# Expert weights split in another slot's step, and a PSUM bank for the z transposes, in a fused attention and mixture-of-experts block

## What is computed

```python
xn = _layernorm(x)
# attention: causal softmax over 256 keys, heads of 16, then Wo and bo
# experts:
scores = sigmoid(xn @ gate_w.T) + bias
topk_w, topk_idx = top_k(scores, 4)
topk_w = topk_w / (sum(topk_w) + 1e-20)
g = einsum('th,eih->eti', xn, Wg);  u = einsum('th,eih->eti', xn, Wu)
z = silu(g) * u
out = einsum('eti,ehi->th', z * cw.T[:, :, None], Wd)
out = out + silu(xn @ Sg.T) * (xn @ Su.T) @ Sd.T
return x + attention(xn) + out
```

## Time and profile before

| | us |
|---|---|
| median of 3 runs (565.2 to 567.9) | 566.04 |
| profiled execution, device time | 569.64 |
| its span | 567.9 |
| loop over slots in it, from the first row transpose to the last output projection | 134 to 554 |

### The profile page before, as it was taken

The page is one execution under the profiler, slowest core; times in us unless marked ns, Lnnn a source line. Parts: engine busy times, 40 slices in busy tenths (PEclk is TensorE's granted clock), DMA queues, the critical chain, the costliest instruction groups (busy, mean ns, idle before and its releaser), DMA issues.

```text
span 567.9 us, 9993 instructions
## 1 busy us (share of the span) xinstructions
PE 468.4 (82%) x2968; PEld 344.9 (61%) x2968; DVE 365.0 (64%) x606; ACT 263.5 (46%) x386; POOL 268.3 (47%) x234
## 2 busy tenths in 40 slices
PE   0995789968989997789878878997978899889880
PEld 0964578846667775367656655765656557667650
DVE  7377874676567957375779871787775546766510
ACT  2531212216555655165668642655736335645610
POOL 2002593304764652267546863573757336364510
PEclk9997999987998998899999899998989999889976
DMA  7804963336666557465687883668655534334222
GB/s 285 329 28 111 226 231 100 107 118 214 158 130 152 113 104 212 142 157 96 141 236 190 277 162 60 154 139 205 175 104 107 95 56 83 68 54 81 38 38 37
DMA packets 32060, 78.23 MB, mean 138 GB/s; under 512 B 4288, under 2 KB 11200, under 8 KB 28800
## 3 DMA queue, kind: packets, MB, share of 16 engines
q0 software_dynamic: 11936, 27.53, 26.8%
q1 hardware_dynamic: 17808, 43.96, 23.5%
q10 hardware_dynamic: 2256, 6.03, 5.0%
HBM read 54.04 MB, written 23.33 MB: 136 GB/s over the span
## 4 chain that ended last, share of the span: by engine, by line
PE 45%; DVE 15%; issue 8%; DMA 8%; ACT 8%; ACTq 6%; POOL 5%; SPq 2%; DVEq 1%; POOLq 1%
PE psum L1093 24%; PE psum L1221 5%; DMA q_parts<-stage 3%; ACT wsplit L573 3%; DVE negm L906 3%; PE psum L1187 2%; PE psum L1203 2%; POOL xn L446 2%; PE psum L1058 2%; ACTq L266 2%; PE psum L1115 2%; PE psum L1042 2%; POOL out L457 1%; PE psum L1103 1%; ACTq L264 1%
## 5 line engine op out<-in xcount | busy, mean ns | idle before, releaser
L1093 PE MATMUL psum<-wsplit,xgT 128*128 (+1 forms) x660 | 175.0, 416 | 0.2
L1093 PEld LDWEIGHTS psum<-wsplit,xgT 128*128 128x128 f32 x660 | 125.8, 197 | 30.3 <-issue 2.7
L457 POOL DMA_INDIRECT out<-ysb,tab x48 | 88.6, 1845 | 105.1 <-ACT ysb L606 84.2
L1093 PE MATMUL psum<-wsplit,zT 128*128 (+1 forms) x336 | 95.3, 420 | 29.0 <-DVE zT L898 29.0
L1093 PEld LDWEIGHTS psum<-wsplit,zT 128*128 128x128 f32 x336 | 61.6, 193 | 48.9 <-issue 37.6
L948 DVE TENSOR_TENSOR xgT<-psum,xgT 128x512 fp32r<-128x512 f32 x47 | 32.3, 688 | 65.4 <-ACT xgT L569 65.3
L437 POOL DMA_INDIRECT xg<-xn_rows,tab x47 | 51.9, 1104 | 29.6 <-PE psum L1231 20.0
L648 ACT ACTIVATE xn<-psum 128x1536 f32<-128x1536 f32 x32 | 46.5, 1453 | 40.6 <-PE psum L1189 40.6
L975 DVE TENSOR_TENSOR plo<-xn,phi 128x1536 f16<-128x1536 f32 x32 | 63.5, 1984 | 1.0
L446 POOL TENSOR_SCALAR_AFFINE_SELECT xn<-xn 128x512 f32<-128x512 f32 x64 | 55.3, 1060 | 7.9 <-ACT xn L648 7.8
L462 POOL TENSOR_TENSOR wsplit<-wraw,wsplit (+1 forms) x16 | 39.1, 2446 | 41.1 <-ACT wsplit L573 41.1
(11 more groups left out here) (180 smaller groups left out, 655.9 us busy)
## 6 DMA issues: line engine op xcount, KB each, us to landing
wraw<-wexp SPq DMA_DIRECT2D x17, 1024.0 KB, 6.1
wraw<-wexp SPq DMA_DIRECT2D x17, 512.0 KB, 4.6
q_parts<-stage SPq DMA_DIRECT2D x16, 192.0 KB
q_pack<-q_parts ACTq DMA_DIRECT2D x6, 384.0 KB, 4.6
xn<-x SPq DMA_DIRECT2D x4, 512.0 KB, 5.2
xn_rows<-xn SPq DMA_DIRECT2D x8, 256.0 KB, 7.6
ctxs<-x SPq DMA_DIRECT2D x8, 256.0 KB, 3.2
out<-ysb SPq DMA_DIRECT2D x8, 256.0 KB, 3.2
```

The costliest lines, as they stand in the source:

```text
L457: nc.gpsimd.indirect_dma_start(out=out, out_offset=rows_of(s), in_=ysb[:, par, :], in_offset=None, compute_op=ALU.add).then_inc(y_out[par] ...
L1093: last = MM(dst, lhs(a, k), split_weights(place, w, c), start=m == 0, stop=m == len(products) - 1)
```

## The change

The table's row 2 now holds, where a slot is the first of expert e, the number e+2, that is the number of the next expert, and 0 for expert 15 and for slots that start none. The gate and up weights of expert e+1 are split in the step of e's first slot: on ACT behind `high16` and ahead of `y_evac` (`gate_up_high`), on DVE behind `low16` at the end of the step (`gate_up_low`). The down weights of that expert follow in the next slot's step, on ACT behind the gate and up halves, if there are any, and on POOL where `down_low_of` stood. A register is loaded once in a slot on each of these engines, behind tanh or `gated`, and kept for the next slot; the parity is worked out from it. `x_high`, `z_high`, `x_low` and `z_low` stand in no branch any more. z is transposed into bank 3, and the wait of PE for y moves from ahead of the z transpose to ahead of `down`. The transposes of maxima in the loop go to bank 4, that of the attention products, with a wait for `csum_done` ahead of them and one for `nmT_sb` ahead of a batch's last `weighted`.

```diff
-        GU, XT, DN, PV = 5, 6, 7, 4
+        GU, XT, DN, PV = 5, 6, 7, 4
+        ZB, NM = 3, PV
...
-            def down_low_of(s):
+            def down_low_of(s, number):
+                if s == 1:
+                    down_low(1, 2)
+                elif s > 1:
+                    with pool.If(number > 0):
+                        down_low(bass.ds((number + 1) % 2, 1), number)
+                    pool.end_ifs()
...
+                        s = SPS * b + j
+                        number = first_of(s - 1) if 1 < s < NSLOT else None
+                        if s < NSLOT:
+                            down_low_of(s, number)
                         add_rows(b, j)
...
+            def gate_up_high(s, number):
+                if s == 0:
+                    weights_high(1, 2, HALVES[0], 0)
+                    weights_high(1, 2, HALVES[1], 0)
+                else:
+                    with act.If(number > 0):
+                        place = bass.ds((number + 1) % 2, 1)
+                        weights_high(place, number, HALVES[0], 0)
+                        weights_high(place, number, HALVES[1], 0)
+                    act.end_ifs()
...
-                        slot_parts(s, 1 - j % 2, not (last and j + 1 >= SPS - 1))
+                        if s + 1 < NSLOT:
+                            x_high(s + 1, 1 - par)
+                        z_high(s + (U1 - 1), 1 - par)
                         if j == BESIDE[g][-1] and (g == 3 or g == 7 and not last):
                             minus_maxima(2 * b + (g // 4 + 1), 1 - g // 4)
+                        if s < NSLOT:
+                            tanh(s + U1, par)
+                        number = first_of(s) if 0 < s < NSLOT else None
                         if j == BESIDE[g][0]:
                             high16(b, g)
+                        if s < NSLOT:
+                            gate_up_high(s, number)
+                            down_high(s, before)
                         y_evac(b, j)
+                        before = number
...
+                own.did(V.tensor_scalar(sexp[:, 0, :], sexp[:, 1, :], float(NE - 1), None, ALU.is_lt))
+                own.wait()
+                op(V.scalar_tensor_tensor(out=sexp_i[:, 2, :], in0=sexp[:, 1, :], scalar=2.0, in1=sexp[:, 0, :],
+                                          op0=ALU.add, op1=ALU.mult))
+                V.tensor_tensor(where[:, 2, :], sexp_i[:, 2, :], sexp_i[:, 1, :], ALU.mult).then_inc(slots_known, 1)
...
-                        slot_parts(s, 1 - j % 2, not (last and j + 1 >= SPS - 1))
-                        if not (last and j == SPS - 1):
+                        if s + 1 < NSLOT:
+                            x_low(s + 1, 1 - j % 2)
+                        z_low(s + (U1 - 1), 1 - j % 2)
+                        if s < NSLOT:
                             gated(s + U1, j % 2)
+                        number = first_of(s) if 0 < s < NSLOT else None
                         if j == BESIDE[g][0] and not (last and g >= 4):
                             maxima(G * b + (g + 4), (g + 4) % G)
                         if j == BESIDE[g][0]:
                             if g:
                                 context(b, g - 1)
                             low16(b, g)
+                        if s < NSLOT:
+                            gate_up_low(s, number)
...
-                        pe.wait_ge(y_sb, s + 1)
+                        if s == 0:
+                            pe.wait_ge(nmT_sb, 1)
                         z_transpose(s + (U1 - 1), 1 - j % 2)
                         if j == BESIDE[g][-1] and (g == 3 or g == 7 and not last):
+                            pe.wait_ge(csum_done, G * b + g + 1)
                             maxima_transpose(G * b + (g + 5), 1 - g // 4)
...
                         pe.wait_ge(w_low[1], prev[1])
+                        pe.wait_ge(y_sb, s + 1)
                         down(s + (U1 - 1), 1 - j % 2, prev[0])
...
                         elif g == G - 1:
+                            if not last:
+                                pe.wait_ge(nmT_sb, 2 * b + 3)
                             weighted(b, g)
```

More of the change, by code:

```diff
@@ L463, in down_low, with first_of @@
                                         wsplit[:, place, 0, PARTS[1]].bitcast(F32), ALU.subtract).then_inc(w_low[1], 1)
-            def down_low_of(s):
[L467 to L471, removed]
+            def first_of(s):
+                return pool.value_load(where[0:1, 2, s + 1:s + 2], min_val=0, max_val=NE)
+            def down_low_of(s, number):
[5 more added lines that the diff above has]
+                    pool.end_ifs()
             def add_attention(b):
@@ L573, in weights_high, with first_of, down_high @@
                 S(wsplit[:, place, 0, cols], wraw[:, place, cols], ACT.Copy).then_inc(w_high[part], 1)
[L575 to L599, removed]
+            def first_of(s):
+                return act.value_load(where[0:1, 2, s + 1:s + 2], min_val=0, max_val=NE)
+            def gate_up_high(s, number):
[8 more added lines that the diff above has]
+                    act.end_ifs()
+            def down_high(s, number):
+                if s == 1:
+                    weights_high(1, 2, PARTS[1], 1)
+                elif s > 1:
+                    with act.If(number > 0):
+                        weights_high(bass.ds((number + 1) % 2, 1), number, PARTS[1], 1)
+                    act.end_ifs()
             def y_evac(b, j):
@@ L659, in context_evac, with sequence @@
                     S(ctxT[:, qt, :, :], bank(qt).rearrange("p (k n) -> p k n", k=KD), ACT.Copy).then_inc(ct_sb, 1)
-            def sequence(b, last):
+            def sequence(b, last, before):
                 for g in range(G):
@@ L894, in shared_out, with z_low @@
                 V.tensor_tensor(ysb[:, n % 2, :], base[:, n % 2, :], bank(DN), ALU.add).then_inc(shared_done, 1)
-            def z_low(n, par, source=DN):
+            def z_low(n, par, source=ZB):
                 dve.wait_ge(zt_high, n + 1)
@@ L954, in gu_low, with first_of, gate_up_low @@
                                 wsplit[:, place, 0, HALVES[half]].bitcast(F32), ALU.subtract).then_inc(w_low[0], 1)
[L956 to L971, removed]
+            def first_of(s):
+                return dve.value_load(where[0:1, 2, s + 1:s + 2], min_val=0, max_val=NE)
+            def gate_up_low(s, number):
+                if s == 0:
+                    gu_low(1, 2, 0)
+                    gu_low(1, 2, 1)
+                else:
+                    with dve.If(number > 0):
+                        gu_low(bass.ds((number + 1) % 2, 1), number, 0)
+                        gu_low(bass.ds((number + 1) % 2, 1), number, 1)
+                    dve.end_ifs()
             def low16(b, g):
@@ L1123, in scores_for_max, with maxima_transpose @@
                     last.then_inc(max_ps, 1)
-            def maxima_transpose(steps, half):
+            def maxima_transpose(steps, half, to=NM):
                 pe.wait_ge(negm_split, steps // 4)
-                TR(psum[0:MROWS * QT * H // 2, 3, 0:P], negm[:, half].rearrange("p c h q -> p (c h q)"),
+                TR(psum[0:MROWS * QT * H // 2, to, 0:P], negm[:, half].rearrange("p c h q -> p (c h q)"),
                    ident[:, :]).then_inc(nmT_ps, 1)
@@ L1169, in _ @@
             pe.wait_ge(rem_done, UNITS)
[L1170 removed]
+            maxima_transpose(4, 0, 3)
             z_transpose(NT - 1, 1, XT)
```

19 lines of the change are left out of this document (8 added, 11 removed).

## The result

| | us |
|---|---|
| before, median of 4 runs (563.98 to 567.9) | 565.62 |
| changed, median of 4 runs (598.98 to 604.65) | 600.95 |
| changed, profiled execution, device time and span | 601.26, 599.5 |
| ratio, 95% interval | 1.063 (1.057 to 1.069) |

The change costs 6.3%, 35 us. The prediction was slower by 11.5 us, at most 28: the sign was right, the size a third of what it is.

A forecast was written before the change was run, and what follows sets the result against it. TensorE's matmuls cover most of the span, so only its idle time and slow stretches could be won. Losses of 38.6 us minus gains of 27.1 gave +11.5 us, 577.5 us from the median 566.04; range 560 to 594.

The forecast's parts named there:

- losses 1 and 2: Gate and up waits for weights split behind `low16`, 14.5 us; GpSimd's down split contending with VectorE's pair, 5 us.
- loss 2: GpSimd's down split meets VectorE's pair at slots 12, 19, 21, 22 and 30: 5 us, 7.2 by the port rule.
- losses 3 and 4: z late behind the split, 8.1 us; down splits moved beside `context` and `low16`, 5.4 us; each with a clock dip.
- Gain 1: No register loads and branches ahead of x on ScalarE: 6.3 us plus three clock dips of 4.2, together 10.5 us.
- gain 3: Splits out of the way of zz and the maxima, so scores and transposes of maxima wait less: 12.2 us.
- first step of the prediction: TensorE idle times of about 2 us bring 3.4 us at 1.2 GHz; each such dip was priced at 1.4 us.
- gain 2: The z transpose no longer waits for ScalarE's evacuation of y (8.0 us of waits): 4.4 us.
- The sum: Losses of 38.6 us minus gains of 27.1 us: 11.5 us slower, chance 0.53.
- (a): Rival: contention, late z and moved down splits cost only their lower bounds, 563 us; chance 0.13.
- (b): Rival: VectorE's seven stalls behind GpSimd's down split, some 12 us, go; faster, 556 us; chance 0.16.
- (c): Rival: ScalarE bounds, with y behind splits delaying exponentials, GpSimd's row add and masks, and fp16 copy; 587 us, chance 0.18.

The follow-up runs named there:

- e5: Changed kernel with GpSimd's down split of experts 2 to 15 cut to 8 of 1024 columns: ratio 1.031 to the kernel before.
- e3: Kernel before with the register part alone: x and z out of the branches, one load per slot and engine, numbering kept: ratio 0.991.
- e6: Changed kernel with both register loads early, ahead of tanh on ScalarE and of `gated` on VectorE: ratio 1.038 to the kernel before.
- e13: Changed kernel with needless bf16 products on TensorE in the five long waits for weights: ratio 1.034 to the kernel before.
- e2: Kernel before with z in bank 3, the wait for y ahead of `down`, and maxima transposes in bank 4 with their waits: ratio 1.002.
- e4: Changed kernel with ScalarE's evacuation of y ahead of both splits instead of behind: ratio 1.066 to the kernel before.
- e11: Changed kernel with gate and up splits and register loads ahead of tanh and `gated`, without the bank and wait changes: ratio 0.989 to the kernel before.

## Why the prediction was right in sign and wrong in size

**Right: which slots, and where the wait comes from.** The eight single-slot experts, and from them that "one ahead" leaves their pairs in the same step but behind `low16`, hold. Waits came at slots 1, 13, 19, 20 and 22, as named, and short ones at 21 and 30: 4.0, 6.5, 4.0, 6.9, 5.7, 2.1 and 2.2 us. The steps of slots 0, 12, 18, 19, 20, 21 and 29 became longer by 26.4 us together in the profiled executions (start to start of gate and up). Of these 3.6 are slow products of slots 19 and 20. The other 22.8 stand against 14.5 + 5 = 19.5 that losses 1 and 2 had without the clock.

**Right: the port.** The five slots of loss 2 are the five whose pairs were stretched, by 2.1 us each. At slots 13, 20 and 22 that stood in the wait, and e5 took 5.9 us from there; I had put 5, with 7.2 as the upper bound. The Trainium skill, "SBUF — State Buffer", section "SBUF: two separate sides", has the pair of ports held for a whole instruction by whichever engine starts first. The trace agrees: GpSimd's split took 2.96 us and ended at 263.47, and VectorE's second half, which began at 261.19, ended at 264.55, 3.36 us where it takes 1.22 alone.

**Right: losses 3 and 4 in their places.** The down product waits for z by 1.1, 4.3, 1.1 and 2.8 us in the steps of slots 7, 23, 27 and 31, where there were 0, 1.8, 0.4 and 0.4, and by 2.5 and 1.5 in those of 8 and 32, where there were 0.5 and 0.

**Gain 1: right in its mechanism, half its size.** The last issue and `xgT` are 0.04 us apart, but the register part is worth 5 us in e3 (3 to 7), against 10.5 that I added up from idle time and three slow stretches.

**Right: gain 3, in the steps that it named.** The steps of slots 5, 17 and 39 to 41 became shorter by 8.7 us together in the changed kernel, against 8.5 that I had put on them; the other 3.7 us of this gain were not taken apart. The scores' waits for the maxima are 7.7 us there only because of the register loads; in e6, with the loads early, 0.8 us of the 5.7 in the earlier trace rows are left:

```profile
PE psum L1208 <- DVE negm L924: 0.8, 4, 0.2
```

**Wrong: the price of the clock, first step of the prediction.** I priced each slow stretch at 1.4 us, from one of 3.4 us. At four of the five waits of 4 us and more it is 6.8 us, and gate and up takes up to 5.34 us. From the first gate and up product of the loop to the last, slow stretches are 58 us in all in the changed kernel and 31 us before. The prediction had 5.6 us for the new ones behind the waits for weights and let the other new and the saved ones nearly cancel; e13 measures 2.9%, 16 us.

**Wrong: the register loads in their new place, put at nothing.** I counted the loads where they were taken away and not where they were put. Gain 1 says "which now stand after tanh" and gives them no price. On VectorE they stand between zz and the maxima and leave 0.23 us of idle time in 21 steps and 0.6 to 1.0 in six more, on ScalarE they stand between tanh and the fp16 copy. The scores wait behind VectorE's. e6 against the changed kernel measures 2.5%, 14 us, against nothing in the sum.

**Wrong: gain 2, 4.4 us.** It was added up from waits as if nothing stood behind each. For the bank part e2 measures nothing: the 8.0 us of waits for y are gone, and 4.6 more ahead of the transposes of maxima, 3.3 for zz and 2.8 for z stand in for them. I had bounded the wait for `csum` at 0.8 us in each of seven steps and then taken zero.

**The sum.** It was 24 us too small. The loads are 14 us of that, gains 1 and 2 together some 10, and the clock 5 to 10 beyond the 5.6 that were taken for it (11 us by the ledger, 16 by e13 alone). That is more than 24, within what the steps are uncertain by. In the steps of the changed kernel the two sides show as well: those of slots 4, 5, 10, 17, 28 and 39 to 41 became shorter, by 16.7 us together. But first-of-group steps that hold no split at all (3, 9, 15, 34, 38) became 0.3 to 1.4 us longer, and those of slots 7 and 8 by 4.7 together. With the loads early (e6) the extra time of 9 and 38 is gone and that of 34 down to 0.4, while 3 and 15 stay 1.1 us longer.

**The rivals.** (a) and (b), which would have made the change neutral or a gain, needed losses 2 to 4 at or near their lower bounds, and none was. (c) had a time of 587 us, nearer than mine, by a mechanism whose first link, y, e4 tests and finds worth nothing: it was near by chance.

**Still open.** Why the steps of slots 3 and 15 stay longer with the loads early was not followed up. How far ScalarE's load works through GpSimd's order (its masks and row adds) or through the fp16 copy alone was not separated.

## What to carry to other kernels

When work is moved within a step, look at what its user does next, not only at how early its unit is prepared: a split made "one unit ahead" that ends a step is just in time for every unit that lasts one step, and eight of sixteen did. Price each idle time of TensorE of 4 us and more with its slow clock behind it: here the five waits of 27 us in all cost 11 to 16 us more. A register load costs where its engine would go straight from one instruction to the next and others wait for the second, so it belongs in front of an instruction that waits anyway. A wait that is taken away is worth no more than the distance to the next late result: look up what else the waiting step needs, as e2 shows. The version to keep is e3, the register part alone, at 0.991 (0.987 to 0.995) of the time before; e11 is equal to it.

## What the runs showed of the hardware

- A wait of TensorE of 4.01 us came with 6.8 us at half clock (gate and up 5.34 us), one of 4.02 us with 3.4 us (gate and up 4.40 us). Before the change, a wait of 1.85 us was followed by 3.4 us at half clock, and one of 1.94 us, which ended at 297.30, by none:

```profile
295.00:302.00 7.00, 5.06 (x43) 3.80 (x39) 6.41 (x10) 4.96 (x7) 5.83 (x5) 1.00 0.78 224
```

- 17 needless bf16 products in the place of the wait of 4.01 us, 3.83 us, kept the clock at 1.00 and gate and up at 3.05 us. With all five long waits filled, by 117 such products, the whole kernel was 2.9% faster.
- VectorE's pair with two inputs from SBUF took 4.50 us with a GpSimd subtraction in between and 2.36 without. GpSimd came 0.45 us into the first half, and it was the second half that was stretched, to 3.36 us: GpSimd got its turn at the end of the first, not after the pair.
- The rows of VectorE's sequencer for its register loads in the changed kernel (duration in ns, min/median/max, then first and last start in us):

```profile
L976 DVEq TENSOR_LOAD <-where x46: 299/306/995, 153.5 to 568.0; - x46
L976 DVEq FUSED_REGOPS  x46: 183/183/209, 154.1 to 568.3; - x46
```

  Such a load of 0.31 us with its 0.18 us of arithmetic behind it, between two VectorE instructions in a row, left 0.23 us of idle time in most cases. With those on ScalarE, 46 on each engine, the late place cost 2.5% of the time before, 14 us, against the idle time that they show themselves (8.9 us on VectorE, 3.2 on ScalarE).
